# First attention of a one-core transformer kernel: four neighbouring distances per GpSimd tile, written back by distance in ScalarE's gelu, GpSimd and VectorE tiles taking turns

## The reference

```python
disp = (x @ W_disp).reshape(B, T, nh, bd)        # 16 heads, 16 values each
strain = disp_win - disp[:, :, :, None, :]       # disp[t-63+d] - disp[t], d = 0..63
bond_act = gelu(strain @ W_strain + rel_emb @ W_pos)
bond_logits = (bond_act @ W_bond)[..., 0]
damage_act = gelu(strain @ W_dmg + b_dmg)
damage = sigmoid((damage_act @ W_dmg_out)[..., 0] + b_dmg_out[0])
logits = bond_logits - 10.0 * damage             # masked before the start of the sequence
weights = softmax(logits)                        # over the 64 distances
out = einsum('bntd,bntde->bnte', weights, val_win)
```

## Time and profile before

| quantity | value |
|---|---|
| time, median of 3 runs | 2834.26 us (2833.05 to 2835.2) |
| the profiled execution's own time | 2835.8 us |
| its span, first to last instruction | 2834.0 us |
| mean granted TensorE clock | 0.925 of full speed |
| TensorE busy | 2320.7 us (82%) |
| VectorE busy | 2215.0 us (78%) |
| ScalarE busy | 1910.5 us (67%) |
| GpSimd busy | 1074.2 us (38%) |
| first attention, first GpSimd tile starts | 31.48 us |
| first attention, last gelu ends | 578.59 us |

### The profile page before, as it was taken

One profiled execution on the slowest core, in us unless ns is written; L12 is line 12 of the kernel. 1 busy time (PEld: TensorE's weight loads), 2 busy tenths in 40 slices (PEclk: granted clock), 3 DMA queues, 4 the chain that ended last, 5 costly groups with the idle time before them and its releaser, 6 DMA issues. The chain is left out here.

```text
span 2834.0 us, 46661 instructions
## 1 busy us (share of the span) xinstructions
PE 2320.7 (82%) x19181; PEld 968.9 (34%) x19181; DVE 2215.0 (78%) x3086; ACT 1910.5 (67%) x1990; POOL 1074.2 (38%) x421
## 2 busy tenths in 40 slices
PE   4677777788846666786699998999879989999996
PEld 2122222255312222243333342333544533333334
DVE  5788888868899999986699838997640358899984
ACT  4999999932643333335499958998432369999981
POOL 5999999912069998932000400004100000000000
PEclk8999999979878988898899999999989989999998
DMA  2011111110034444401311020002010030110000
GB/s 78 1 45 45 57 53 66 50 56 8 26 130 164 163 161 150 163 9 46 76 21 29 13 43 1 13 13 50 8 42 0 22 84 16 44 34 19 16 9 27
DMA packets 67166, 145.55 MB, mean 51 GB/s; under 512 B 13683, under 2 KB 30431, under 8 KB 66240
## 3 DMA queue, kind: packets, MB, share of 16 engines
q1 hardware_dynamic: 66944, 142.47, 17.2%
HBM read 117.99 MB, written 24.25 MB: 50 GB/s over the span
## 5 line engine op out<-in xcount | busy, mean ns | idle before, releaser
L828 POOL TENSOR_TENSOR l0a_diff_pool<-l0a_A,l0a_a_of_t 128x2048 f32<-128x2048 f32 x128 | 531.7, 4202 | 31.2 <-ACT l0a_a_of_t L843 30.7
L2124 ACT ACTIVATE l2x_pT<-ps 128x1024 f32<-128x1024 f32 x512 | 470.2, 1165 | 13.3 <-PE ps L2082 13.3
L2276 ACT ACTIVATE l3he_pT<-ps 128x1024 f32<-128x1024 f32 x480 | 445.2, 1062 | 18.4 <-PE ps L2210 18.4
L1438 PE MATMUL ps<-l1s_hc,all_ident 128*128 128x512 f32 x512 | 285.1, 710 | 155.2 <-POOL l1s_hc L1409 100.8
L774 DVE SCALAR_TENSOR_TENSOR l0a_diff_dve<-l0a_A,l0a_pos,ps 128x512 f32<-128x512 f32 x512 | 344.7, 740 | 30.3 <-PE ps L619 30.2
L1400 POOL TENSOR_TENSOR l1s_dBx<-l1a_dtx,l1a_Bs 128x1024 f32<-128x1024 f32 x128 | 297.5, 2354 | 111.9 <-POOLq L1134 111.9
L1424 ACT ACTIVATE ps<-l1a_dt,l1a_A 128x1024 f32<-128x1024 f32 x128 | 143.1, 1118 | 268.0 <-DVE l1s_hc L1483 215.7
L2082 PE MATMUL ps<-l2m_Qs,l2m_Ks 75*32 75x512 bf16 x4096 | 274.0, 386 | 13.3 <-DMA l2m_Qs<-l2m_mparts 9.0
L2210 PE MATMUL ps<-l3h_Qs,l3h_Ks 75*32 75x512 bf16 x4096 | 274.9, 384 | 9.9 <-DVE ps L2281 9.9
L2097 PE MATMUL ps<-l2x_pT,l2m_Va 128*9 128x512 f32 x2048 | 270.0, 598 | 8.4 <-DVE l2s_oT L2690 3.0
L860 ACT ACTIVATE l0a_diff_pool<-l0a_diff_pool 128x2048 f32<-128x2048 f32 x128 | 237.3, 1901 | 25.8 <-POOL l0a_diff_pool L828 25.7
(11 more groups left out here) (493 smaller groups left out, 3672.3 us busy)
## 6 DMA issues: line engine op xcount, KB each, us to landing
l1a_Bs<-l1a_bc SPq DMA_DIRECT2D x64, 512.0 KB, 3.6
l1s_Cs<-l1a_bc SPq DMA_DIRECT2D x64, 512.0 KB, 4.6
l0a_band_rows<-l0a_band SPq DMA_DIRECT2D x32, 512.0 KB, 6.6
l0a_band<-l0a_exps SPq DMA_DIRECT2D x14, 512.0 KB
l2m_Ks<-l2m_parts SPq DMA_DIRECT2D x36, 128.0 KB
l2m_Qs<-l2m_parts SPq DMA_DIRECT2D x72, 64.0 KB
l3h_Qs<-l3h_parts SPq DMA_DIRECT2D x72, 64.0 KB
l0a_band<-l0a_zero SPq DMA_DIRECT2D x8, 512.0 KB, 7.4
```

The costliest lines, as they stand in the source:

```text
L828: pool.tensor_tensor(out, window(s), atb[:, p % 2, :].unsqueeze(1).broadcast_to([P, 4, CH]), ALU.subtract).then_inc(diff_pool, 1)
L1438: mm = pe.matmul(g.ps[:, (4 + 2 * h + q) * CH:(5 + 2 * h + q) * CH], g.ident[:, :], hc[:, m % NHC, q * CH:(q + 1) * CH], start=(n == 0), s ...
L2124: act.activation(pT[:, turn % NPT, :], g.ps[:, slot * QC:(slot + 1) * QC], ACT.Exp).then_inc(expd, 1)
L2276: act.activation(pT[:, (4 * m + j) % NPT, :], g.ps[:, slot(turn)], ACT.Exp).then_inc(expd, 1)
```

## The change

The order of tiles in a group becomes k = 0, 1, 0, 1, ...: GpSimd and VectorE tiles take turns. Tile n now holds the four neighbouring distances 16·dg + 4n + c, so the four windows start one element apart. VectorE's tiles keep the layout distance by time. GpSimd's tiles are laid out time by distance: for each token four elements in a row, from four neighbouring elements of A, less one element of `atb` that is read four times. ScalarE's gelu of such a tile reads it with a step of four elements (16 bytes) and writes it distance by time into a second pair of buffers. Where GpSimd had four buffers in and out, it has two for its own output, freed by the gelu, and two for the gelu's output, freed by TensorE. The tanh of a group moves behind the first gelu of the next group, `logits` moves from offset 5 to 7, and the logits are turned round by a matmul with a permuted identity (`by_row`, made once by one VectorE copy), as the rows of the banks now stand in another order of distances.

```diff
-    ND, NP_, NBT = 4, 4, 4
-    D_AT = (4, 5, 6, 7)
+    ND, NPI, NPO, NBT = 4, 2, 2, 4
+    PER = TPG // 2
...
+                    dve.tensor_copy(by_row[:, :].rearrange("p (n c h) -> p c n h", n=4, c=4), g.ident[:, :].rearrange("p (c n h) -> p c n h", c=4, n=4))
...
-        dp = r.sb("diff_pool", [P, NP_, 4, CH])
+        dpi = r.sb("diff_pool", [P, NPI, CH, 4])
+        dpo = r.sb("gelu_pool", [P, NPO, 4, CH])
...
-            k, n = divmod(rest, 4)
+            n, k = divmod(rest, 2)
...
-            first = A[:, hf, k, q * CH + 16 * dg + n + 1:q * CH + 16 * dg + n + 2]
-            return bass.AP(first.tensor, first.offset, [list(first.ap[0]), [4, 4], [1, CH]])
+            first = A[:, hf, k, q * CH + 16 * dg + 4 * n + 1:q * CH + 16 * dg + 4 * n + 2]
+            return bass.AP(first.tensor, first.offset, [list(first.ap[0]), [1, 4], [1, CH]])
...
-                        mm = pe.transpose(out[:, dg * P:(dg + 1) * P], L[:, p % 2 * GPP + dg, b * P:(b + 1) * P], g.ident[:, :])
+                        mm = pe.matmul(out[:, dg * P:(dg + 1) * P], L[:, p % 2 * GPP + dg, b * P:(b + 1) * P], by_row[:, :], start=True, stop=True)
...
-                    if off % TPG == 5 and 0 < w * GPP + off // TPG <= NT // TPG:
+                    if off % TPG == 7 and 0 < w * GPP + off // TPG <= NT // TPG:
...
-                        dve.wait_ge(reduced, (i - ND) // ND * TPG + D_AT[i % ND] + 1)
+                        dve.wait_ge(reduced, s - 2 * ND + 1)
                     src = window(s)
                     for c in range(4):
-                        d = 16 * dg + 4 * c + n
+                        d = 16 * dg + 4 * n + c
...
-                    if i >= NP_:
-                        pool.wait_ge(reduced, (i - NP_) // NP_ * TPG + i % NP_ + 1)
-                    pool.tensor_tensor(out, window(s), atb[:, p % 2, :].unsqueeze(1).broadcast_to([P, 4, CH]),
-                                       ALU.subtract).then_inc(diff_pool, 1)
+                    if i >= NPI:
+                        pool.wait_ge(gelu_done, s - 2 * NPI + 1)
+                    pool.tensor_tensor(dpi[:, i % NPI, :, :], window(s).rearrange("p c t -> p t c"),
+                                       atb[:, p % 2, :].unsqueeze(2).broadcast_to([P, CH, 4]), ALU.subtract).then_inc(diff_pool, 1)
...
+                def tanh(gi):
+                    act.wait_ge(reduced, TPG * gi + TPG - 1)
+                    if gi >= 2:
+                        act.wait_ge(logit_done, gi - 1)
+                    act.activation(th[:, gi % 2, :], bank(2), ACT.Tanh, bias=hb[:, :], scale=0.5).then_inc(tanh_done, 1)
...
-                    if s % TPG == 6:
-                        gi = s // TPG
-                        act.wait_ge(reduced, TPG * gi + 4)
...
-                    ge, sem, i = slot(s)
-                    act.wait_ge(sem, i + 1)
-                    act.activation(ge, ge, ACT.Gelu).then_inc(gelu_done, 1)
+                    if s % TPG == 1 and s > TPG:
+                        tanh(s // TPG - 1)
+                    ge, i = slot(s)
+                    if k:
+                        act.wait_ge(diff_dve, i + 1)
+                        act.activation(ge, ge, ACT.Gelu).then_inc(gelu_done, 1)
+                    else:
+                        act.wait_ge(diff_pool, i + 1)
+                        if i >= NPO:
+                            act.wait_ge(reduced, s - 2 * NPO + 1)
+                        act.activation(ge, dpi[:, i % NPI, :, :].rearrange("p t c -> p c t"), ACT.Gelu).then_inc(gelu_done, 1)
+                tanh(NT // TPG - 1)
```

More of the change, by code:

```diff
@@ L344, in bond_attention @@
         early = r.sb("early_mask", [P, W])
+        by_row = r.sb("distance_of_row", [P, P])
         band = nc.dram_tensor("l0a_band", [2, 4, P, UB * HH], F32, kind="Internal").ap()
@@ L502, in slot @@
         def slot(s):
-            i = s // TPG * len(D_AT) + D_AT.index(s % TPG) if s % TPG in D_AT else s // TPG * NP_ + s % TPG
-            return (dd[:, i % ND, :, :], diff_dve, i) if s % TPG in D_AT else (dp[:, i % NP_, :, :], diff_pool, i)
+            i = s // 2
+            return (dd[:, i % ND, :, :], i) if s % 2 else (dpo[:, i % NPO, :, :], i)
         def place(s):
@@ L613, in _ @@
                     p, q, hf, dg, k, n = place(s)
-                    ge, _, _ = slot(s)
+                    ge, _ = slot(s)
                     pe.wait_ge(gelu_done, s + 1)
@@ L679, in a_of_t @@
                     if p:
-                        dve.wait_ge(diff_dve, len(D_AT) * GPP * p)
+                        dve.wait_ge(diff_dve, PER * GPP * p)
                     dve.tensor_copy(bank(1), A[:, hf, 1, at]).then_inc(at_ready, 1)
@@ L763, in _ @@
                     tail(p, s % TPP)
-                    if s % TPG not in D_AT:
+                    if k == 0:
                         continue
-                    out, _, i = slot(s)
-                    if s % TPP == D_AT[0]:
+                    out, i = slot(s)
+                    if s % TPP == 1:
                         dve.wait_ge(at_ready, p + 1)
                     if i >= ND:
-                        dve.wait_ge(reduced, (i - ND) // ND * TPG + D_AT[i % ND] + 1)
+                        dve.wait_ge(reduced, s - 2 * ND + 1)
                     src = window(s)
                     for c in range(4):
-                        d = 16 * dg + 4 * c + n
+                        d = 16 * dg + 4 * n + c
                         ins = dve.scalar_tensor_tensor(out[:, c, :], src[:, c, :], pos[:, d:d + 1], bank(1), ALU.add, ALU.subtract)
@@ L820, in _ @@
                     p, q, hf, dg, k, n = place(s)
-                    if s % TPG in D_AT:
+                    if k:
                         continue
-                    out, _, i = slot(s)
+                    _, i = slot(s)
                     if s % TPP == 0:
                         pool.wait_ge(atb_ready, p + 1)
-                    if i >= NP_:
-                        pool.wait_ge(reduced, (i - NP_) // NP_ * TPG + i % NP_ + 1)
-                    pool.tensor_tensor(out, window(s), atb[:, p % 2, :].unsqueeze(1).broadcast_to([P, 4, CH]),
-                                       ALU.subtract).then_inc(diff_pool, 1)
+                    if i >= NPI:
+                        pool.wait_ge(gelu_done, s - 2 * NPI + 1)
+                    pool.tensor_tensor(dpi[:, i % NPI, :, :], window(s).rearrange("p c t -> p t c"),
+                                       atb[:, p % 2, :].unsqueeze(2).broadcast_to([P, CH, 4]), ALU.subtract).then_inc(diff_pool, 1)
             @block.scalar
@@ L841, in a_of_t_sbuf @@
                     if p >= 2:
-                        act.wait_ge(diff_pool, (p - 1) * GPP * NP_)
+                        act.wait_ge(diff_pool, (p - 1) * GPP * PER)
                     act.activation(atb[:, p % 2, :], A[:, hf, 0, PAD + q * CH:PAD + (q + 1) * CH], ACT.Identity,
                                    bias=nbd[:, :]).then_inc(atb_ready, 1)
+                def tanh(gi):
[3 more added lines that the diff above has]
+                    act.activation(th[:, gi % 2, :], bank(2), ACT.Tanh, bias=hb[:, :], scale=0.5).then_inc(tanh_done, 1)
                 a_of_t_sbuf(0)
@@ L851, in _ @@
                         exps(p - 1)
-                    if s % TPG == 6:
-                        gi = s // TPG
-                        act.wait_ge(reduced, TPG * gi + 4)
-                        if gi >= 2:
-                            act.wait_ge(logit_done, gi - 1)
-                        act.activation(th[:, gi % 2, :], bank(2), ACT.Tanh, bias=hb[:, :], scale=0.5).then_inc(tanh_done, 1)
-                    ge, sem, i = slot(s)
-                    act.wait_ge(sem, i + 1)
-                    act.activation(ge, ge, ACT.Gelu).then_inc(gelu_done, 1)
+                    if s % TPG == 1 and s > TPG:
+                        tanh(s // TPG - 1)
+                    ge, i = slot(s)
+                    if k:
+                        act.wait_ge(diff_dve, i + 1)
[6 more added lines that the diff above has]
+                tanh(NT // TPG - 1)
                 for b in range(LB):
```

## The result

| | before | after |
|---|---|---|
| time, median of 4 runs each on one chip | 2833.66 us | 3066.3 us (3062.27 to 3072.31) |
| ratio, 95% interval | | 1.0823 [1.0807, 1.0839] |
| span of the profiled execution | 2834.0 us | 3060.4 us |
| last gelu of the first attention ends | 578.59 us | 808.69 us |

The change makes the kernel 8.2% slower, by 232.6 us. I had forecast 2810, a gain of 24. The last gelu of the first attention comes 230.1 us later, and the profiled spans differ by 226.4, so the whole loss lies in this stage.

A forecast was written before the change was run, and what follows sets the result against it. GpSimd was taken as the bound, ScalarE close behind. The profiled 2835.8 us less a net gain of 24.5 gave 2811.3, and 1.5 less for the median 2809.8, in round terms 2810; range 2803 to 2868.

The forecast's parts named there:

- What bounds the kernel: First attention: GpSimd sets the pace at 67.2 us a phase, ScalarE close behind at 65.0.
- The most a faster GpSimd can give: First attention: ScalarE's idle time between first and last gelu goes, net 24.5 us.
- GpSimd's instruction: GpSimd's subtraction in the new layout: taken as 3.8 us a tile, between 3.82 and 5.3 as ends.
- ScalarE's gelu of these tiles: Gelu reading GpSimd's tiles with a 16-byte step: taken as unchanged at 1.90 us; 1.24 times would cost +30 us.
- Rival C: ScalarE's strided gelu is dearer: 2865 us at 1.24 times, 3040 at twice; chance 0.18.
- Rival A: GpSimd's new instruction is no cheaper than the present mean (4.0 to 4.25 us): 2843 us; chance 0.17.
- B: GpSimd's new instruction is dearer, 4.3 us and more: 2877 us at 4.5; chance 0.17.
- D: TensorE's lag or two-deep buffers make ScalarE wait, with the cheap GpSimd instruction: 14 us given back, 2824; chance 0.08.
- Order and buffers: GpSimd stalls at exponentials, 16 us at the present pitch, hidden at 3.8; the stage's end saves 7.6 if GpSimd stays bound.

The follow-up runs named there:

- e1: Changed kernel, but ScalarE's gelu of GpSimd's tiles reads and writes in one plain run, so TensorE reduces elements in the wrong order; 2808.98 us, 0.9915.
- e4: Changed kernel, but GpSimd itself writes its elements out by distance (2 KB apart) and the gelu is plain; 2806.92 us, 0.9904.
- e7: e4's kernel with the gelu in place and one set of four buffers freed by TensorE's reduction instead of two and two; 2806.3 us, 0.9898.
- e10: Kernel before's tiles, new order, gelu in place, four buffers; GpSimd's tiles 0 and 3 subtract a second, shifted copy VectorE makes from PSUM; 2802.61 us, 0.988.
- e5: Changed kernel, but GpSimd's tiles are distance by time as before, gelu plain; neighbouring windows, new order and two plus two buffers stay; 2844.74 us, 1.0027.
- e3: Changed kernel, but the gelu is plain, its output stays time by distance, and TensorE's matmuls read with a step of 16 bytes; 2836.92 us, 1.0008.
- e9: Kernel before's tiles (distances four apart, distance by time) in the new order, gelu in place, four buffers freed by TensorE; 2824.48 us, 0.9964.
- e6: Kernel before with its old order, four buffers and in-place gelu, but neighbouring distances and GpSimd's new instruction writing by distance; 2833.0 us, 0.9997.

## Why the prediction was wrong

**What bounds the kernel: right.** GpSimd was the bound and ScalarE close behind. Once GpSimd is faster, and nothing else slower (e1, e4, e7, e10), ScalarE is busy 99.9 of 100 us.

**The most a faster GpSimd can give: right.** The 24.5 us became about 24 in e1 (ratio 0.9915, 19 to 29 us by its interval).

**GpSimd's instruction: right in sign, better in size.** 3.60 us where I took 3.8, and all tiles alike (3.599 to 3.604). My guess that two streams cross a multiple of four elements together pointed at the right thing, their relative position; the price by itself shows that it is the distance of the two inputs, and that the output has no part. The upper bounds from GpSimd's strided memset (4.5 to 5.3) fell: this instruction writes its output in a row, and no price near theirs appeared, not even in e4, where it writes with a step (3.98).

**ScalarE's gelu of these tiles: here it failed.** "I take no change" was wrong by a factor of two: 3926 ns for 1901, 260 us of an engine that had 24.8 to give. The step read three rows amiss. VectorE's maximum with and without a step (682 and 682) reads PSUM; I wrote "though from PSUM" and leaned on it all the same, and PSUM turned out to be exempt (ScalarE 597 at any step, from SBUF 1107). TensorE's loads at 0.52 against 0.42 are weight loads; its moving stream, which is what resembles a gelu's input, goes from 610 to 1077 ns at the same step. GpSimd's memset, the one SBUF row that showed a larger price, became an upper end, which I then set aside with no reason given. Worst was the last sentence of the step, that ScalarE asks less of SBUF per ns than TensorE does: that compared rates of plain access, while what is paid is one access to 16 bytes for each element.

**Rival C: right, and priced too low in chance and at its end.** Its "twice" gave 3040; the measured 3066 is 26 higher, as the gelu's step from start to start is 3.82 us on average, 2.02 more and not 1.80 more: 128 × 0.22 = 28 us. By its condition, that each element is on a new line, nothing in this kernel spoke against it but the PSUM row and the weight loads' 1.24. I gave it 0.18 and left the part from 1.34 times out of the range. Where SBUF rows are split and the only flat one is of another memory, this rival deserved about as much as the forecast, and the range had to reach past 3040.

**Rival A: right as a sum.** It was not the case, as the instruction is cheaper, but e5 built its condition and took 2844.7 for the 2843, with stalls of 17.7 us for the 16. **Rivals B and D** did not come: no dearer GpSimd (even with the stepped write 3.98), and in e1 ScalarE waits for no reduction. D's mechanism does appear in e3, where TensorE's reading is slower: 26 us of ScalarE's waits, 28 us of time over e1.

**Order and buffers: right on the stall, too high on the end, and missed on one point.** The end gave 5.2 us in e9 where I had 7.6. And I had counted the new order as worth no more than that, while e6 shows that the faster GpSimd gives nothing without it: ScalarE then waits 18.4 us for VectorE's tiles in the place of GpSimd's.

## What to carry to other kernels

Before a transposing access is added, look for a row of the same kind of memory and the same stream: in SBUF an instruction whose neighbouring elements each lie in 16 bytes of their own took 1.8 to 2.1 times as long on ScalarE and on TensorE's moving side and 1.4 to 1.5 times on VectorE, and an engine without slack pays that in full. If the turn has to be made, make it where it is cheap or hidden (here GpSimd's write, 0.06 us a tile alone and 0.38 in the kernel), or out of PSUM. And an engine that shows 99% busy after a change is a success only if it also runs more instructions in the same time.
